# Last stage of a graph network: three bf16 pieces against two float32r pieces with a widened adjacency

## The reference, cut to what matters

```python
# third layer, twice: mean over incoming edges, then two dense terms
neigh = segment_sum(h[src], dst) / max(deg, 1)
h = h @ W_self.T + neigh @ W_neigh.T + b          # relu after the first one
# fourth layer, three times (widths 128 -> 256 -> 256 -> 128)
out = segment_sum(h[src_f] * norm[:, None], dst_f) + b   # with self loops
h = layer_norm(relu(out), g, be)
```

## Time and profile before

| | us |
|---|---|
| median of 3 runs | 3863.35 (3851.28 to 3868.51) |
| the profiled execution, its own time | 3844.19 |
| its span, first to last instruction | 3842.3 |
| last stage (3065 to the end), span | 777 |
| TensorE busy over the span | 3290.5 (86%) |
| mean granted TensorE clock | 0.942 |

### The profile page before, as it was taken

One profiled execution on the slowest core, in us unless ns is written; L12 is line 12 of the kernel. 1 busy time (PEld: TensorE's weight loads), 2 busy tenths in 40 slices (PEclk: granted clock), 3 DMA queues, 4 the chain that ended last, 5 costly groups with the idle time before them and its releaser, 6 DMA issues. The chain is left out here.

```text
span 3842.3 us, 81259 instructions
## 1 busy us (share of the span) xinstructions
PE 3290.5 (86%) x22381; PEld 2019.8 (53%) x22381; DVE 1831.5 (48%) x5337; ACT 1453.3 (38%) x3467; POOL 1784.3 (46%) x1807
## 2 busy tenths in 40 slices
PE   3999989974776999996888888688888789999998
PEld 1666666653554565653555554344444445555554
DVE  4676767766653444442444444344444332352222
ACT  3555555541272454542333333133333231131112
POOL 1554555530026777773777777377777500000000
PEclk8999999997898999998999899689999989999999
DMA  4677777656556666664878788477777555442223
GB/s 120 187 213 201 213 200 198 187 146 160 176 148 173 170 184 176 184 176 122 228 215 232 208 219 223 114 210 213 201 207 209 139 178 183 174 143 98 71 106 122
DMA packets 717296, 675.29 MB, mean 176 GB/s; under 512 B 383127, under 2 KB 543713, under 8 KB 716885
## 3 DMA queue, kind: packets, MB, share of 16 engines
q1 hardware_dynamic: 623366, 466.26, 41.6%
q0 software_dynamic: 77008, 200.24, 19.9%
q10 hardware_dynamic: 16768, 6.91, 0.7%
HBM read 530.84 MB, written 142.28 MB: 175 GB/s over the span
## 5 line engine op out<-in xcount | busy, mean ns | idle before, releaser
L2199 POOL DMA_INDIRECT l_y<-s_lrows,l_src x1332 | 1331.4, 1000 | 443.4 <-issue 381.7
L3202 PE MATMUL ps<-nl_adj,nl_table 126*128 126x504 bf16 (+1 forms) x3150 | 631.8, 357 | 2.3 <-DVE nl_table L3437 2.3
L960 POOL DMA_INDIRECT em_gs<-s_rows,em_idx x400 | 392.6, 982 | 352.9 <-DMA em_idx<-in_sd 240.8
L2239 PE MATMUL ps<-ident,l_y 128*128 128x128 f32 x1800 | 270.7, 287 | 226.0 <-DMA l_y<-s_lrows,l_src 142.7
L3202 PEld LDWEIGHTS ps<-nl_adj,nl_table 126*128 126x128 bf16 x3150 | 301.9, 96 | 299.3 <-issue 6.0
L2593 DVE TENSOR_TENSOR l_y<-l_y 128x768 f32<-128x768 f32 x225 | 214.1, 952 | 368.4 <-DMA l_y<-s_lrows,l_src 327.2
L2282 PE MATMUL ps<-l_y,aw_pT 128*63 128x277 f32 x2700 | 375.3, 415 | 2.5 <-ACT aw_pT L2476 1.7
L2462 ACT ACTIVATE aw_yT<-ps 128x512 f32<-128x512 f32 (+1 forms) x525 | 261.6, 534 | 277.6 <-PE ps L2239 268.8
L2239 PEld LDWEIGHTS ps<-ident,l_y 128*128 128x128 f32 x1800 | 206.7, 145 | 285.8 <-issue 221.7
L2266 PE MATMUL ps<-aw_yT,aw_qt 128*63 128x384 f32 x1800 | 335.2, 495 | 6.3 <-DMA aw_yT<-s_dxT 6.3
L2476 ACT ACTIVATE aw_pT<-ps 128x381 f32<-128x381 f32 x225 | 110.1, 489 | 460.4 <-PE ps L2274 446.4
(11 more groups left out here) (375 smaller groups left out, 5759.4 us busy)
## 6 DMA issues: line engine op xcount, KB each, us to landing
nl_adj<-s_adj SPq DMA_DIRECT2D x20, 3100.8 KB
aw_yT<-s_dxT SPq DMA_DIRECT2D x150, 384.0 KB, 4.4
aw_geoS<-s_geoS SPq DMA_DIRECT2D x450, 94.5 KB
nl_adj<-s_adj SPq DMA_DIRECT2D x15, 2325.6 KB
ws_msg<-s_msg SPq DMA_DIRECT2D x75, 384.0 KB, 3.8
s_dxT<-aw_yT SPq DMA_DIRECT2D x75, 384.0 KB, 2.9
aw_qt<-s_qt SPq DMA_DIRECT2D x225, 126.0 KB
s_msg<-em_msg SPq DMA_DIRECT2D x100, 256.0 KB, 2.9
```

The source lines that it names most:

```text
L960: pool.indirect_dma_start(out=gs[:, u, j, :], out_offset=None, in_=d["rows0"], in_offset=bass.IndirectOffsetOnAxis(ap=idx[:, u, 2 * j:2 * ...
L2199: pool.indirect_dma_start(out=y[:, u, j, 0:W], out_offset=None, in_=table, in_offset=bass.IndirectOffsetOnAxis(ap=src[:, u, j:j + 1], axis ...
L2239: m = nc.tensor.transpose(k.ps[:, FEATURES[n], q * 128:(q + 1) * 128], y[:, u, j, what * D:(what + 1) * D], k.ident[:, :])
L3202: m = nc.tensor.matmul(k.ps[:, bank(i, p), 0:cols * WN], source[:, p, q, b, :], adj[:, a % 2, 0:cols, b * WN:(b + 1) * WN], start=b == 0 a ...
```

## The change

The features of the last stage are held as two float32r pieces in place of three bf16 ones: DVE cuts each row's bits to its upper 12 significant ones (`MASK`, a bitwise and with -4096), ACT copies that into the table (`HIGH`), and DVE writes row minus mask (`LO`). `REST` and `MID` go. `aggregate` does two matmuls per block, both operands float32r. The adjacency stays bf16 in DRAM and is widened to float32r in SBUF: a turn's matrix comes in `NPC` = 5 pieces of 5 source blocks (`PB`), each loaded into one of three bf16 buffers (`raw`) and copied by GpSimd into one of four float32r buffers (`adj`). TensorE waits for each piece (`cast`) and gives it back (`consumed`). For c2 the order is piece by piece, both halves of a piece one after the other. The places of `make`, `turn` and `mix` in the order are moved. SP issues all small loads first, then 175 loads of pieces, each behind the copy of three pieces before. The earlier stage writes A in the layout of pieces: 5 runs of 420 bytes per partition and window where there was one of 2100. `rows(i)` of DVE waits for its own last step of the turn before, and `MASK` for `HIGH` of the turn before.

```diff
@@ edge_messages, store_window
-                sp.dma_start(d["adj"][bass.ds(i * NWI + v, 1), :, :].rearrange("w p c -> (w p) c"),
-                             adj[:, v, 0:NB, :].rearrange("p b n -> p (b n)")).then_inc(adj_out[v], 16)
+                sp.dma_start(d["adj_pieces"][:, :, bass.ds(i * NWI + v, 1), :].rearrange("n p w c -> p (n w) c"),
+                             adj[:, v, 0:NB, :].rearrange("p (n b) m -> p n (b m)", b=PB)).then_inc(adj_out[v], 16)
@@ node_layers
-    DVE_ROUND = ((0, "SUM"), (0, "NEG"), (0, "CEN"), (2, "REST"), (1, "REC"), (1, "Y"), (2, "LO"))
-    ACT_ROUND = ((-1, "KEEP"), (0, "SQ"), (1, "ROOT"), (2, "MID"), (1, "HIGH"))
+    DVE_ROUND = ((0, "SUM"), (0, "NEG"), (0, "CEN"), (1, "REC"), (1, "Y"), (1, "MASK"), (1, "LO"))
+    ACT_ROUND = ((-1, "KEEP"), (0, "SQ"), (1, "ROOT"), (2, "HIGH"))
-        table = [sb("table0", [BM, 1, 3, NB, D], BF16), sb("table1", [BM, 2, 3, NB, D], BF16)]
-        adj = sb("adj", [BM, 2, AW, NB * WN], BF16)
+        table = [sb("table0", [BM, 1, 2, NB, D], F32R), sb("table1", [BM, 2, 2, NB, D], F32R)]
+        RING, RAW = 4, 3
+        adj = sb("adj", [BM, RING, AW, PB * WN], F32R)
+        raw = sb("raw", [BM, RAW, AW, PB * WN], BF16)
@@ sync
-                if a >= 2:
-                    sp.wait_ge(summed, a - 1)
-                sp.dma_start(adj[:, a % 2, 0:n, :], d["adj"][w:w + n, :, :].rearrange("w m q -> m w q")).then_inc(adj_in[a % 2], 16)
-            load(AHEAD)
+                for p in range(NPC):
+                    g = NPC * (i - AHEAD) + p
+                    if g >= RAW:
+                        sp.wait_ge(cast, g - RAW + 1)
+                    sp.dma_start(raw[:, g % RAW, 0:n, :], d["adj_pieces"][p, :, w:w + n, :]).then_inc(raw_in[g % RAW], 16)
...
@@ gpsimd
+            for i in range(AHEAD, len(turns)):
+                n = 3 * SIZES[turns[i][1]]
+                for p in range(NPC):
+                    g = NPC * (i - AHEAD) + p
+                    pool.wait_ge(raw_in[g % RAW], 16 * (g // RAW + 1))
+                    if g >= RING:
+                        pool.wait_ge(consumed, g - RING + 1)
+                    nc.gpsimd.tensor_copy(adj[:, g % RING, 0:n, :], raw[:, g % RAW, 0:n, :]).then_inc(cast, 1)
@@ tensor, aggregate
+                order = [(n, p, b) for n in range(NPC) for p in range(parts) for b in range(n * PB, (n + 1) * PB)]
+                for at, (n, p, b) in enumerate(order):
+                    g = NPC * a + n
+                    if p == 0 and b == n * PB:
+                        pe.wait_ge(cast, g + 1)
-                    for q in range(3):
+                    for q in range(2):
                         m = nc.tensor.matmul(k.ps[:, bank(i, p), 0:cols * WN], source[:, p, q, b, :],
-                                             adj[:, a % 2, 0:cols, b * WN:(b + 1) * WN],
+                                             adj[:, g % RING, 0:cols, b % PB * WN:(b % PB + 1) * WN],
...
-                    if was != "x" and n == (8 if was == "c1" else 2):
+                    if was != "x" and at == (12 if was == "c1" else 3):
                         make(i - 1)
-                    if was == "c3" and n == 18:
+                    if was == "c3" and at == 23:
                         turn(i - 1)
-                    if was == "c2" and n == (30 if kind == "c2" else 19):
+                    if was == "c2" and at == (45 if kind == "c2" else 19):
                         turn(i - 1)
-                    if was == "c2" and n == (38 if kind == "c2" else 20):
+                    if was == "c2" and at == (49 if kind == "c2" else 20):
                         mix(i - 1)
@@ scalar, rows: HIGH copies the mask; MID is gone
-                    nc.scalar.activation(hi, src, ACT.Copy).then_inc(s, 1)
-                    act.wait_ge(dve_.sem, dve_.of(i, "REST"))
-                    nc.scalar.activation(mid, low, ACT.Copy).then_inc(s, 1)
+                    act.wait_ge(dve_.sem, dve_.of(i, "MASK"))
+                    nc.scalar.activation(hi, top_, ACT.Copy).then_inc(s, 1)
@@ vector, rows
+                dve.wait_ge(s, dve_.of(i - 1, "RES" if turns[i - 1][0] == "c3" else "LO"))
...
-                nc.vector.tensor_tensor(low, src, hi, ALU.subtract).then_inc(s, 1)
-                dve.wait_ge(act_.sem, act_.of(i, "MID"))
-                nc.vector.tensor_tensor(lo, low, mid, ALU.subtract).then_inc(s, 1)
+                dve.wait_ge(act_.sem, act_.of(i - 1, "HIGH"))
+                nc.vector.tensor_scalar(top_.bitcast(I32), src.bitcast(I32), TOP12, None, ALU.bitwise_and).then_inc(s, 1)
+                after("MASK")
+                nc.vector.tensor_tensor(lo, src, top_, ALU.subtract).then_inc(s, 1)
```

More of the change, by code:

```diff
@@ L9 @@
 I16 = mybir.dt.int16
+F32R = mybir.dt.float32r
 ALU = mybir.AluOpType
@@ L48 @@
 MOST = 256
+PB = 5
+NPC = NB // PB
+TOP12 = -4096
 KEY0 = 8192
@@ L3004, in node_layers @@
     DVE_STEPS = dict(
[L3005 to L3008, removed]
+        n0=["SCALE", "SELF", "BIAS", "MASK", "LO"],
+        n1=["SCALE", "SELF", "BIAS", "RES", "SUM", "NEG", "CEN", "REC", "RD", "Y", "MASK", "LO"],
+        c1=["SCALE", "BIAS", "NEG", "CEN", "REC", "Y", "GAIN", "SHIFT", "NEXT", "MASK", "LO"],
+        c2=["SCALE", "BIAS", "NEG", "CEN", "REC", "Y", "GAIN", "SHIFT", "NEXT", "MASK", "LO"],
         c3=["SCALE", "BIAS", "NEG", "CEN", "REC", "Y", "GAIN", "SHIFT", "RES"])
     ACT_STEPS = dict(
[L3011 to L3014, removed]
+        n0=["TAKE", "RELU", "HIGH"],
+        n1=["TAKE", "SQ", "ROOT", "HIGH"],
+        c1=["TAKE", "RELU", "SQ", "ROOT", "HIGH"],
+        c2=["TAKE", "RELU", "SQ", "ROOT", "HIGH"],
         c3=["TAKE", "RELU", "SQ", "ROOT"])
-    DVE_ROUND = ((0, "SUM"), (0, "NEG"), (0, "CEN"), (2, "REST"), (1, "REC"), (1, "Y"), (2, "LO"))
-    ACT_ROUND = ((-1, "KEEP"), (0, "SQ"), (1, "ROOT"), (2, "MID"), (1, "HIGH"))
+    DVE_ROUND = ((0, "SUM"), (0, "NEG"), (0, "CEN"), (1, "REC"), (1, "Y"), (1, "MASK"), (1, "LO"))
+    ACT_ROUND = ((-1, "KEEP"), (0, "SQ"), (1, "ROOT"), (2, "HIGH"))
     def each(i, step):
@@ L3207, in aggregate @@
+                    if b % PB == PB - 1 and p == parts - 1:
+                        m.then_inc(consumed, 1)
                     if b == 0 and kind in LOOPS:
                         for j in range(SIZES[c]):
-                            for q in range(3):
+                            for q in range(2):
                                 nc.tensor.matmul(k.ps[:, bank(i, p), j * BM:(j + 1) * BM], source[:, p, q, FIRST[c] + j, :],
-                                                 idb[0:BM, 0:BM], start=False, stop=False)
+                                                 idr[:, :], start=False, stop=False)
@@ L3317, in deviation @@
                 nc.scalar.activation(std[:, i % 2, 0:nb], squares[:, i % 2, 0:nb], ACT.Sqrt, bias=k.eps[0:BM, 0:1], scale=1.0 / D).then_inc(s, 1)
-            def middle(i):
-                act.wait_ge(dve_.sem, dve_.of(i, "REST"))
-                nc.scalar.activation(table[0][:, 0, 1, blocks(turns[i][1]), :], beyond_high(i), ACT.Copy).then_inc(s, 1)
             def high(i):
-                act.wait_ge(dve_.sem, dve_.of(i, "Y"))
-                nc.scalar.activation(table[0][:, 0, 0, blocks(turns[i][1]), :], rows_of(i), ACT.Copy).then_inc(s, 1)
+                act.wait_ge(dve_.sem, dve_.of(i, "MASK"))
+                nc.scalar.activation(table[0][:, 0, 0, blocks(turns[i][1]), :], top(i), ACT.Copy).then_inc(s, 1)
             keep(0)
@@ L3455, in normalise, with cut @@
                                                ALU.max, ALU.mult).then_inc(s, 1)
[L3457 to L3464 removed]
+            def cut(i):
+                dve.wait_ge(s, dve_.of(i, "Y"))
+                if i >= 2:
+                    dve.wait_ge(act_.sem, act_.of(i - 2, "HIGH"))
+                nc.vector.tensor_scalar(top(i).bitcast(I32), rows_of(i).bitcast(I32), TOP12, None, ALU.bitwise_and).then_inc(s, 1)
+                dve.wait_ge(s, dve_.of(i, "MASK"))
+                nc.vector.tensor_tensor(table[0][:, 0, 1, blocks(turns[i][1]), :], rows_of(i), top(i), ALU.subtract).then_inc(s, 1)
             for n in range(AHEAD + 2):
```

78 lines of the change are left out of this document (29 added, 49 removed).

## The result

The changed kernel takes 3897.1 us (3893.89 to 3909.3, four runs) against 3862.51 (3851.28 to 3868.51) beside it: a ratio of 1.0099, 95% interval 1.0067 to 1.0131. The forecast was 3783 in a range of 3710 to 3950. The time lies in the range, but on the side that had a chance of 0.34.

A forecast was written before the change was run, and what follows sets the result against it. TensorE was taken to bound the kernel, except c1, a loop through three engines. Long turns sum to -14.8 us, times 6.25 is -92, plus 12 at layer changes: -80 from 3863 gives 3783 us, range 3710 to 3950.

The forecast's parts named there:

- the side that had a chance of 0.34: Whole kernel: the change makes it slower; faster had 0.60 and same 0.06.
- `store_window`: Stage that builds A: 37,800 more runs add a DMA share of 0.16 to 0.75; taken nothing, at most +10 us.
- The copies' length: GpSimd's copies in the last stage: 0.813 ns an element, 2.23 or 1.72 us a copy, 11.2 us a long turn.
- The rival of 1.49 ns: GpSimd's copies at the upper bound, 3.85 us a copy, 19.3 us a long turn; 3946 us in all, chance 0.12.
- A copy adds 2.05 us to an instruction with two SBUF inputs that falls behind it: Last stage, VectorE beside GpSimd: they take turns; listed BIAS, CEN, Y, GAIN, SHIFT, RES, LO and c1's NEXT.
- copies and five such instructions of 512 elements ... 13.9. Taken: 15: Layer n1's long turn: 11.2 us of copies plus 5 x 0.53 on one port; 15 us taken, from 18.04.
- the port costs more: Last stage: five copies each fall ahead of a DVE instruction on the path, 10 us a turn; 3897 us, chance 0.11.
- The float32r step, 0.217 taken: Last stage's sums: a float32r matmul of 504 columns steps like bf16; a long turn loses 5.43 us per half.
- the rival of 4050: Last stage's matmuls: float32r at the float32 record's column rate, 0.426 us at 504 columns, +187 us; chance 0.16.
- Full gain: Last stage: the change saves all that TensorE's count says, 204 us, giving 3660 us; chance 0.03.
- x, "Nothing; at most +9": Turns x of the last stage: first piece, issued behind the small loads, is ready at 3103; nothing lost, at most +9 us.

The follow-up runs named there:

- experiment 2: The changed kernel with A stored as before (one run of 2100 bytes), each load picking its piece out of the rows; 3843.82 us, ratio 0.9979.
- experiment 3: The changed kernel with only the first four copies whole and every later copy one element, so later turns use old pieces of A; 3799.35 us, ratio 0.9845.
- Experiment 5: The kernel before, with GpSimd making the same 175 copies of its adjacency into a buffer that nobody reads; 3921.77 us, ratio 1.0161.
- experiment 1: The kernel before with only A's layout changed to pieces, loaded back by five DMAs a turn, no copies; 3916.98 us, ratio 1.016.
- experiment 12: The changed kernel with old layout of A, first three loads early, copies of two windows in c1 and c3, thirds elsewhere; 3794.43 us, ratio 0.9831.

## Why the prediction was wrong, step by step

**`store_window`: "Still under TensorE ... Taken: nothing, at most +10".** This is the step that turned the sign: +57.5 in the trace, 49.5 to 53 by experiment 2. The price itself was well bounded (50 ns for each added run; 13 measured, 154 - 103 over four). The mistake was to set it against TensorE's 92%. An engine that is 92% busy does not show that what feeds it has slack. Before the change TensorE already waited 42.9 us of 600 for the gather, and that wait was in the trace to be read. DMA's share of 0.75 was a mean over a stage in which the gather was at times the last to come. Nor is this step the whole miss: without it, experiment 2 comes out 0.2% faster, where 2% were forecast. The rest lies in the layers.

**The copies' length: right.** 2.23 and 1.72 us were forecast, the shortest are 2.279 and 1.757, so 0.83 ns an element. The rival of 1.49 ns is refuted.

**"A copy adds 2.05 us to an instruction with two SBUF inputs that falls behind it": right in kind, too narrow in list and too small for n1.** `NEG` and `MASK` belong to the list; `SCALE` and `SELF`, which read PSUM, kept their lengths, as the prediction said. By layer the copies were taken at 15 us in n1 (2.4 a long turn), 34 in c1 (5.5), 2.5 in c2 (0.4) and 25 in c3 (4). Measured, with and without copies (kernel after against experiment 3), they cost 40, 35, 6 and 27. So c1 and c3 were right, and n1 is the term that was mis-sized. It was costed as work on one port, "copies and five such instructions of 512 elements ... 13.9. Taken: 15", which TensorE's 12.6 nearly covers. The trace has a chain instead, in which four steps of VectorE stand behind a copy each, 6.9 us in the turn shown. Periods of long turns, forecast and measured: n1 15 and 17.7 to 20.2; c1 23 and 23.1 to 25.3; c3 17 and 15.8 to 20.4. The rival "the port costs more" has n1 21, c1 28, c3 20 and c2 33; n1 and c3 come near it, c2 does by the float32r step, and c1 stays near the forecast. That its 3897 is the measured time to the us is luck: its own long turns (13.5 for n0 as in the forecast) sum to +2.2 and not +3.5 us, which makes 3889, and 57.5 us of the measured time are another stage's.

**The float32r step, 0.217 taken: 0.241 at 504 columns.** From the chain of the kernel after, in n0 and then in c2:

```profile
3224.59 8.20 PE ps L3220 x34
...
3612.25 19.33 PE ps L3220 x80
```

Both give 0.241 us at a granted clock of 1.00, 1.11 times bf16's 0.217, also at 1.00, and far from the float32 record's 0.426; the rival of 4050 is refuted. (The Trainium skill, page "SBUF — State Buffer", in its table of bandwidths, has two bytes a lane and cycle for bf16; read as a limit of the port, as the prediction did, it would double the step, and this trace disagrees.) A long turn has 50 such steps, 1.2 us more, c2 2.4: n0 13.5 became 14.1, c2 30 became 32.2. With 6.25 long turns that is (0.6 + 2.2) x 6.25, some 17 us on the path in n0 and c2. The identities take 0.105 us each (0.84 for 8, L3228 in the same chain), near the upper bound.

**"Full gain", 3660: refuted.** Even without copies the last stage takes 639.0 us, not 762 - 204 = 558, since the step and the chains of c1 and of the layers' changes remain (TensorE still waits 15 us in c1 and 9 in c3).

**x, "Nothing; at most +9": +13.8.** The first piece is issued at 3149.84, behind the small loads, and its copy starts at 3160.35, 10.5 us later where 4.4 was taken; then six copies in a row, 14.48 us, stand in the way of x's vector work:

```profile
3149.84 15.43 SPq L3111 DMA_DIRECT2D nl_raw<-s_adj_pieces  x5
...
3160.35 14.48 POOL L3136 CAST nl_adj<-nl_raw 126x2520 fp32r<-126x2520 bf16 x6 [26.86 <-DMA nl_raw<-s_adj_pieces]
```

Experiment 5 has the same +13.7 from copies alone, with its loads where they were; I had left x out of the list of layers that the copies meet. But the parts don't add up: experiment 3, with only the first four copies whole, still has +8.5, and experiment 1, with none, +11. What share is the copies' and what the late or split loads' stays open.

**The balance.** 3783 forecast, 3897 measured, against kernels before of 3863: 114 us. In the traces the miss is 130: the store's stage 57.5, the stages between 3, x 14, and the layers 56. Of the layers' 56 the copies are some 27 (107 us for 80 taken, n1 alone 40 for 15), and the other 29 are what the layers without copies take above the forecast, mainly the float32r step. The lower clock of the last stage (0.89 for 0.96) is inside these parts; its share isn't settled. That the medians show 16 us less than the traces is the spread between executions: the trace of the kernel before was 18 us under its median, that of the kernel after 3.

## What to carry to other kernels

Ask of a stage which wait ends last there, not how busy its busiest engine is: DMA time added to a stage whose matmuls already wait on a gather came through 1.1 to 2.0 times, the clock falling with the waits. Keep the runs of such a store at 1 KB, and let the reader pick the pieces. Work given to an idle GpSimd is paid by VectorE by the instruction, so cost it as waits along VectorE's chain and not as a sum of work on the port; three shorter copies beat one, and very short ones in an unbroken row did not beat those.

## What the hardware showed beyond that

- An addition of VectorE was held for up to 14.71 us until a row of 48 copies of 420 elements ended, while with copies of 2520 elements it waited for one. The Trainium skill, page "SBUF — State Buffer", has the shared port pair as a lock held for the full instruction; by that rule the wait would end with the copy under way. The traces agree for long copies and not for rows of short ones. Why it was `BIAS` nearly each time (one more, of 4.6 us, was that of c3 in experiment 12), behind a read of PSUM, is open.
- `NEG`, 126 x 4 elements with one input, takes 1034 ns on average beside copies and 172 without, and `MASK` of 512 elements 1129 for 428, so these two wait as well. The reciprocal (178 ns) and the reduction (686 ns), also with one SBUF input, never did, nor did any instruction that reads PSUM.
- A float32r matmul's step is 0.241 us at 504 columns, 0.182 at 378 and 0.105 at 126, where bf16's is 0.217 at 504 and 0.163 at 378, at a granted clock of 1.00.
- A widening DMA (bf16 to float32r) moved 221 GB/s of float32 bytes on 16 busy engines; a piece of 1240 KB landed 17.2 us after its issue.
